# A causal mask by TensorE in the cross-attention stage, masked keys as one exponent per row, and no identity products between the transposes

## The chip, the cores and the metric

One core of a Trainium2 chip runs the whole program in one launch. The metric is the device time of the program in microseconds (us), the median of several runs. Engines: PE (TensorE), DVE (VectorE), ACT (ScalarE), POOL (GpSimd), and SP, which issues transfers.

## The reference, cut to what matters

Two layers, each an attention and a feed-forward part. The change is in the attention of the second layer: 8 batch rows, 256 queries and 256 keys, 512 features, 16 heads of 32. Queries are the normalised x; keys and values are the context itself, without projections.

```python
x = x + jnp.tanh(g_xattn[1]) * _L1_xattn_ref(_layernorm(x, axis=-1), ctx_2048, ctx_2048)
# in _L1_xattn_ref, with HEADS = 16, MASKED_BIAS = -10000.0:
scores = jnp.einsum('bhqd,bhkd->bhqk', qh, kh) / math.sqrt(hd)
causal = ki <= qi
scores = jnp.where(causal[None, None], scores, jnp.asarray(MASKED_BIAS, scores.dtype))
attn = jax.nn.softmax(scores, axis=-1)
out = jnp.einsum('bhqk,bhkd->bhqd', attn, vh)
```

The mask is -10000 and not minus infinity, so a masked key keeps a (tiny) share exp(-10000 - maximum), which the kernel computes too.

## The kernel before, in words

The program is seven stages, one after the other, with a barrier of all engines between them. The change is in stage 6, the function `cross`. It works on the eight batch rows in turns of two; in the code `b` is the row of a turn (a "batch" below, eight of them in all), `t` one of its two tiles of 128 queries, `h` a head, and `p` a pair of heads. A batch is eight steps `i`, one pair each. All engines run the same chain of steps (`chain` calls the `step(i, at, batch)` of each engine), in the order that their `step` functions write out; nothing but semaphores ties them together. Each engine executes its own instructions in order.

In a step with pair p:

- PE (`scores`, L1755 and L1758): four products with 32 rows, two heads by two query tiles, into the PSUM tensor `S[p % 2]` (two banks). The first query tile gets only its own 128 keys, the second all 256. It first waits until the exponentials of pair p-2 are done, since they read the same `S`. Then `turn_probs` for the second head of pair p-2, in even steps `values` (L1782, sixteen products for the four heads of two pairs), and `turn_probs` for the first head of pair p-1. `turn_probs` first multiplies the identity by itself into a part of the bank that nobody reads (L1764, two instructions in the trace), then waits for the head's exponentials, and turns three 128x128 blocks of probabilities (L1767).
- DVE (`maximum`): writes -10000 over the masked places of the two diagonal blocks of both heads with a predicated copy (L1915), then takes the negated maximum of each row (L1919).
- ACT: `exps` for the first head of pair p-1 (L1844, L1846, with the row sums), `keep_probs` (L1857, the copy of turned probabilities from PSUM) for the second head of pair p-2, `exps` for the second head of pair p-1, `keep_probs` for its first head.

Once a batch there is more. The first query tile's keys 128 to 255 are all masked and were never scored; their share is one exponent per row and head (`exps_apart`, L1851), times the sum of those keys' values, which PE makes with a product of ones by the second half of the context (`second_values`, L1743, step 1, into the PSUM bank `M`) and DVE copies out (L1910). DVE adds that share to the sums, inverts them (`over_sums`, L1926 to L1933, step 1); POOL makes `ev` from it (L1693) and adds it to x (`xe`, L1699, step 3), and adds the outputs (`y`, L1706, steps 4 and 5). DVE also takes the next batch's layer norm statistics (L192 to L197, step 2), normalises it (L204, step 4), scales the outputs (L1940, steps 3 and 4) and copies the second half of the next queries (L1905, step 6). PE turns the outputs (L1792, steps 3 and 4) and the next x (L1737, steps 5 and 6) through the same bank `M`. SP loads at step 1 and stores at step 6. Before the first steps PE runs 12 identity products at a time (L253).

## Time and profile before

| | |
|---|---|
| median of 3 runs | 2247.9 us (2247.34 to 2250.03) |
| the profiled execution: its own time, its span | 2249.69, 2247.9 us |
| mean granted clock of PE | 0.963 |
| busy over the span: PE, DVE, ACT, POOL | 89%, 61%, 48%, 19% |
| the cross stage, from 1828 to 2070.7 us: PE, DVE, ACT, POOL busy | 209.98, 182.65, 175.32, 51.68 us |

The profile is of one execution of the program. "Busy" is the time in which an engine has an instruction at work; PE's matmuls overlap and their ends are modelled, so a group of them can last longer in the trace than until the next group starts. Starts are therefore better to read than durations on PE. Behind a line of a timeline stands, in brackets, how long the engine idled before it and what released it. The granted clock (PEclk) is a share of 2.4 GHz, 0.50 is the lower level of 1.2 GHz.

### The profile page before, as it was taken

What the parts mean: (1) busy time and instruction counts of PE and PEld (TensorE: products, weight loads), DVE (VectorE), ACT (ScalarE), POOL (GpSimd) and SP (SyncE); (2) the same over time, 40 slices, a digit from 0 to 9 for tenths busy, and PEclk for the clock granted to TensorE, in tenths of its full rate; (3) what the DMA queues carried; (4) which work ended last, traced back from release to release, by engine and by line L of the source; (5) the groups of instructions that cost most, each with busy time, mean ns of one, the idle gap of its engine ahead of it and who ended that gap; (6) DMA issues with size and microseconds to landing.
All of it is one profiled execution on the core that took longest, in us unless ns stands there. A gap on an engine that the chain in (4) does not pass through costs nothing. (4 is left out here: it accounts for less than half of the span.)

```text
span 2247.9 us, 33557 instructions
## 1 busy us (share of the span) xinstructions
PE 1996.2 (89%) x10802; PEld 1531.6 (68%) x10818; DVE 1371.1 (61%) x2400; ACT 1073.3 (48%) x2593; POOL 425.4 (19%) x504
## 2 busy tenths in 40 slices
PE   6999479999989999987997999999689979997898
PEld 5888357776767677766886778778578866665454
DVE  6777266666666666663323764554544328885786
ACT  3333156666656666653113412121134318885898
POOL 1111034444444444430000000000000001222110
PEclk9999789999999999998998999999899989998999
DMA  5665662323232321006443221112295322321111
GB/s 213 243 243 231 244 178 76 98 64 103 60 101 76 85 76 48 22 27 239 145 136 137 83 75 38 56 37 57 62 339 198 118 81 68 113 94 48 48 56 43
DMA packets 192217, 250.42 MB, mean 111 GB/s; under 512 B 11574, under 2 KB 143814, under 8 KB 181836
## 3 DMA queue, kind: packets, MB, share of 16 engines
q1 hardware_dynamic: 192076, 248.67, 33.9%
q8 instruction: 72, 1.18, 0.2%
q14 instruction: 69, 0.57, 0.1%
HBM read 152.14 MB, written 96.48 MB: 111 GB/s over the span
## 5 line engine op out<-in xcount | busy, mean ns | idle before, releaser
L930 ACT ACTIVATE at_prob<-at_S,at_bias,at_rq 128x384 f32<-128x384 f32 (+1 forms) x256 | 184.2, 731 | 165.3 <-DVE at_bias L1016 159.1
L1027 DVE TENSOR_TENSOR at_pt_lo<-at_PT,at_pt_hi 128x512 fp32r<-128x512 f32 x224 | 148.8, 688 | 92.6 <-ACT at_pt_hi L937 92.6
L798 POOL TENSOR_SCALAR at_prob<-at_prob,at_rsum 128x384 f32<-128x384 f32 (+1 forms) x256 | 160.3, 639 | 174.7 <-DVE at_rsum L1022 174.7
L1444 ACT ACTIVATE gu_silu<-gu_G 128x512 f32<-128x512 f32 x64 | 38.3, 598 | 269.6 <-PE gu_G L103 260.1
L857 PE MATMUL at_PT<-c_ident,at_prob 128*128 128x128 f32 x896 | 127.8, 277 | 44.1 <-DVE at_pt_lo L1027 44.1
L937 ACT ACTIVATE at_pt_hi<-at_PT 128x512 fp32r<-128x512 f32 x224 | 127.9, 604 | 53.1 <-PE at_PT L857 53.1
L1007 DVE TENSOR_REDUCE at_nmax<-at_S 128x1 f32<-128x384 f32 (+1 forms) x256 | 147.7, 615 | 4.7 <-PE at_S L850 4.2
L857 PEld LDWEIGHTS at_PT<-c_ident,at_prob 128*128 128x128 f32 x896 | 97.7, 140 | 75.6 <-DVE at_pt_lo L1027 71.2
L1477 DVE TENSOR_TENSOR gu_h<-gu_silu,gu_U 128x512 f32<-128x512 f32 x64 | 43.9, 687 | 154.6 <-PE gu_U L103 109.7
L846 PE MATMUL at_S<-at_k_hi,at_q_hi 128*128 128x384 f32 (+1 forms) x256 | 112.7, 440 | 16.6 <-DVE at_q_lo L1032 13.4
L789 POOL TENSOR_TENSOR at_rq<-at_qv,c_minus_half 128x4 f32<-128x4 f32 x64 | 65.1, 1017 | 288.0 <-DVE at_qv L1002 288.0
L101 PE MATMUL gu_G<-gu_n_hi,gu_g_hi 128*128 128x512 f32 x256 | 103.0, 402 | 14.2 <-DVE gu_n_lo L1466 14.2
L101 PE MATMUL at_Q<-at_wq_hi,at_xt_hi 128*128 128x512 f32 x256 | 108.4, 423 | 7.1 <-issue 4.2
L213 POOL TENSOR_TENSOR x_rstd<-x_ve,c_minus_half 128x2 f32<-128x2 f32 x8 | 9.0, 1121 | 520.0 <-DVE x_ve L197 520.0
L101 PE MATMUL gu_U<-gu_n_hi,gu_u_hi 128*128 128x512 f32 x256 | 101.0, 395 | 5.9 <-DVE gu_h L1477 4.6
L103 PE MATMUL at_Q<-at_wq_lo,at_xt_hi 128*128 128x512 f32 x256 | 103.2, 403 | 0.0
L1172 PE MATMUL d_Y<-d_w_hi,d_a_hi 128*128 128x512 f32 x256 | 101.6, 397 | 1.7 <-DVE d_a_lo L1263 1.7
L102 PE MATMUL at_Q<-at_wq_hi,at_xt_lo 128*128 128x512 f32 x256 | 102.6, 401 | 0.0
L103 PE MATMUL gu_G<-gu_n_lo,gu_g_hi 128*128 128x512 f32 x256 | 102.6, 401 | 0.0
L102 PE MATMUL gu_G<-gu_n_hi,gu_g_lo 128*128 128x512 f32 x256 | 102.5, 401 | 0.0
L1172 PE MATMUL o_Y<-o_w_hi,o_a_hi 128*128 128x512 f32 x256 | 99.8, 390 | 1.7 <-DVE o_a_lo L1263 1.7
L102 PE MATMUL gu_U<-gu_n_hi,gu_u_lo 128*128 128x512 f32 x256 | 100.3, 392 | 0.0
(272 smaller groups left out, 5658.5 us busy)
## 6 DMA issues: line engine op xcount, KB each, us to landing
wide<-at_ot SPq DMA_DIRECT2D x64, 256.0 KB, 2.9
wide<-gu_h SPq DMA_DIRECT2D x64, 256.0 KB, 3.2
o_a<-wide SPq DMA_DIRECT2D x14, 1024.0 KB, 4.8
d_a<-wide SPq DMA_DIRECT2D x14, 1024.0 KB, 4.8
keys_hi<-kv_kt_hi SPq DMA_DIRECT2D x8, 1024.0 KB, 4.0
keys_lo<-kv_kt_lo SPq DMA_DIRECT2D x8, 1024.0 KB, 6.0
values_hi<-kv_v_hi SPq DMA_DIRECT2D x8, 1024.0 KB, 8.0
values_lo<-kv_v_lo SPq DMA_DIRECT2D x8, 1024.0 KB, 9.6
```

The costliest lines, as they stand in the source:

```text
L101: pe.matmul(out, wh, xh, start=(start and k == 0), stop=False)
L102: pe.matmul(out, wl, xh, start=False, stop=False)
L103: last = pe.matmul(out, wh, xl, start=False, stop=(stop and k == len(terms) - 1))
L789: pool.tensor_tensor(rq[u % 4][:], qv[u % 2][:], c.minus_half[:, 0:GROUP], ALU.pow).then_inc(rq_ready.sem, 1)
L798: pool.tensor_scalar(prob[u % 2][:, h, 0:n], prob[u % 2][:, h, 0:n], rsum[:, s:s + 1], 1.0, ALU.mult, ALU.mult).then_inc(normed.sem, 1)
L846: pe.matmul(S[h][:, 0:n], q_hi[u % 2][:, own], keys, start=True, stop=False)
L857: last = pe.transpose(bank_of("p", u, kb)[:, h * P:(h + 1) * P], prob[u % 2][:, h, kb * P:(kb + 1) * P], c.ident[:])
L930: act.activation(prob[u % 2][:, h, 0:n], S[h][:, 0:n], ACT.Exp, bias=bias[:, s:s + 1], scale=rq[u % 4][:, h:h + 1], accum_out=sums[:, s:s ...
L937: act.activation(pt_hi[f % 4][:], bank_of("p", u, kb)[:], ACT.Copy).then_inc(pt_hi_done.sem, 1)
L1007: dve.tensor_reduce(nmax[:, s:s + 1], S[h][:, 0:blocks[u] * P], AX_X, ALU.max, negate=True).then_inc(max_done.sem, 1)
L1027: dve.tensor_tensor(pt_lo[f % 4][:], bank_of("p", u, kb)[:], pt_hi[f % 4][:].bitcast(F32), ALU.subtract).then_inc(pt_done.sem, 1)
L1172: pe.matmul(Y[r][:], a_hi[r][:, k, :], w_hi[:, k, :], start=(k == 0), stop=False)
```

## The change: what it does

- The mask is added on PE: after the four score products of a pair, two bf16 products of the identity by a table of 0 and -1e30 (one per head, 256 columns, both diagonal blocks) accumulate onto `S`, and only the second signals DVE. The predicated copy goes.
- The maximum is followed by a small operation that bounds it (128x4, `tensor_scalar`), so that a row with masked keys has a maximum of at least -10000.
- All masked keys of both query tiles are now taken apart: the exponent per row and head has 32 columns in place of 16, times a count per row; their values are sums over the later keys (`masked_values`: a table `later` by the context, one product more for the first tile), so three fp32 products of 512 columns a batch on PE in place of one, in steps 1 and 2, two copies on DVE in place of one, and `ev` and `xe` on POOL for both tiles.
- The identity products in `turn_probs` go (128 in all). Those of L253 stay.
- Tables are made on DVE at the start of the stage, and one more is loaded.

```diff
-        apart = mem.sb("apart", [P, H1])
-        apart_gain = mem.sb("apart_gain", [P, H1])
-        v1 = [mem.sb(f"v1_{b}", [P, D]) for b in range(2)]
+        apart = mem.sb("apart", [P, QT, H1])
+        apart_gain = mem.sb("apart_gain", [P, QT, H1])
+        vm = [mem.sb(f"vm{b}", [P, QT, D]) for b in range(2)]
         ev = mem.sb("ev", [P, D])
-        xe = mem.sb("xe", [P, D])
+        xe = mem.sb("xe", [P, QT, D])
         ot = mem.sb("ot", [P, DC, L])
         o = [mem.sb(f"o{i}", [P, D]) for i in range(2)]
         y = mem.sb("y", [P, TT, D])
         after = mem.sb("after", [P, P], I32)
-        masked = mem.sb("masked", [P, 4 * P])
+        after_f = mem.sb("after_f", [P, P])
+        later = mem.sb("later", [P, P])
+        mask_f = mem.sb("mask_f", [P, P])
+        mask = mem.sb("mask", [P, P], BF16)
+        count = mem.sb("count", [P, QT])
+        bound = mem.sb("bound", [P, 1])
+        masked = mem.sb("masked", [P, 1])
...
+            sp.dma_start(mask_f[:], io["c_diag_mask"]).then_inc(setup, 16)
...
-            def add_apart(turn, b):
+            def add_apart(turn, b, t):
                 by_head = "p (h d) -> p h d"
+                n = QT * b + t
                 pool.wait_ge(*apart_gained.at(turn, b + 1))
-                pool.wait_ge(*v1_kept.at(turn, b + 1))
-                pool.wait_ge(*xe_done.at(turn, b))
-                pool.tensor_tensor(ev[:].rearrange(by_head, h=H1), v1[b][:].rearrange(by_head, h=H1),
-                                   apart_gain[:].rearrange("p (h a) -> p h a", a=1).to_broadcast([P, H1, HD1]),
+                pool.wait_ge(*vm_kept.at(turn, n + 1))
+                pool.wait_ge(*xe_done.at(turn, n))
+                pool.tensor_tensor(ev[:].rearrange(by_head, h=H1), vm[b][:, t, :].rearrange(by_head, h=H1),
+                                   apart_gain[:, t, :].rearrange("p (h a) -> p h a", a=1).to_broadcast([P, H1, HD1]),
                                    ALU.mult).then_inc(ev_done.sem, 1)
-                pool.wait_ge(*ev_done.at(turn, b + 1))
+                pool.wait_ge(*ev_done.at(turn, n + 1))
                 pool.wait_ge(*x_arrived[b].at(turn, 16))
-                pool.wait_ge(*y_done.at(turn, QT * (b - 1) + 1))
-                pool.tensor_tensor(xe[:], x[:, QT * b, :], ev[:], ALU.add).then_inc(xe_done.sem, 1)
+                pool.wait_ge(*y_done.at(turn, n + 1 - QT))
+                pool.tensor_tensor(xe[:, t, :], x[:, n, :], ev[:], ALU.add).then_inc(xe_done.sem, 1)
             def add(turn, b, t):
                 if t == 0:
-                    pool.wait_ge(*xe_done.at(turn, b + 1))
                     pool.wait_ge(*y_stored[b].at(turn, 0))
+                pool.wait_ge(*xe_done.at(turn, QT * b + t + 1))
                 pool.wait_ge(*o_done.at(turn, QT * b + t + 1))
-                pool.tensor_tensor(y[:, QT * b + t, :], o[t][:], xe[:] if t == 0 else x[:, QT * b + 1, :],
-                                   ALU.add).then_inc(y_done.sem, 1)
+                pool.tensor_tensor(y[:, QT * b + t, :], o[t][:], xe[:, t, :], ALU.add).then_inc(y_done.sem, 1)
             def step(i, at, batch):
                 if i == 2:
                     for turn, b in batch(1):
                         ln.gpsimd(pool, turn, c.minus_half, b)
-                if i == 3:
+                if i in (2, 3):
                     for a in batch(-1):
-                        add_apart(*a)
+                        add_apart(*a, i - 2)
                 if i in (4, 5):
...
-                    pe.wait_ge(*v1_kept.at(turn, b))
+                    pe.wait_ge(*vm_kept.at(turn, QT * b))
...
-            def second_values(turn, b):
-                pe.wait_ge(*cx_arrived[b].at(turn, 16))
-                pe.matmul(M[:], c.ones[:], cx[:, QT * b + 1, :], start=True, stop=True).then_inc(V1_full.sem, 1)
+            def masked_values(turn, b, t):
+                if t == 0:
+                    pe.wait_ge(*cx_arrived[b].at(turn, 16))
+                    pe.wait_ge(*x_kept[1].at(turn, b + 1))
+                else:
+                    pe.wait_ge(*vm_kept.at(turn, QT * b + 1))
+                last = pe.matmul(M[:], later[:], cx[:, QT * b + t, :], start=True, stop=(t == 1))
+                if t == 0:
+                    last = pe.matmul(M[:], c.ones[:], cx[:, QT * b + 1, :], start=False, stop=True)
+                last.then_inc(VM_full.sem, 1)
...
-                              start=True, stop=True)
+                              start=True, stop=False)
                 for a in range(2):
-                    last = pe.matmul(S[p % 2][:, 2 * L * a + L:2 * L * (a + 1)], qt[b][rows[a], k, P:L],
-                                     kt[b][rows[a], k, :], start=True, stop=True)
+                    pe.matmul(S[p % 2][:, 2 * L * a + L:2 * L * (a + 1)], qt[b][rows[a], k, P:L],
+                              kt[b][rows[a], k, :], start=False, stop=False)
+                for a in range(2):
+                    diagonals = S[p % 2][:, 2 * L * a:2 * L * (a + 1)].rearrange("p (t l) -> p t l", t=QT)[:, :, 0:P]
+                    last = pe.matmul(diagonals, c.ident_bf[:],
+                                     mask[:].rearrange("p (a l) -> p a l", a=1).to_broadcast([P, QT, P]),
+                                     start=False, stop=True)
                 last.then_inc(S_full.sem, 1)
             def turn_probs(turn, h):
                 pe.wait_ge(*pt_done.at(turn, h - 1))
-                pe.matmul(PT[h % 2][:, 3 * P:4 * P], c.ident[:], c.ident[:], start=True, stop=True)
                 pe.wait_ge(*exp_done.at(turn, h + 1))
                 for stands, block in ((0, 0), (2, 1), (1, 2)):
...
-                if i == 1:
-                    for turn, b in batch(0):
-                        pe.wait_ge(*x_kept[1].at(turn, b + 1))
-                        second_values(turn, b)
+                if i in (1, 2):
+                    for a in batch(0):
+                        masked_values(*a, i - 1)
                 if i == 3:
                     for a in batch(-1):
                         for turn, b in batch(0):
-                            pe.wait_ge(*v1_kept.at(turn, b + 1))
+                            pe.wait_ge(*vm_kept.at(turn, QT * (b + 1)))
...
+            pe.wait_ge(tables, 7)
             chain(pe, step)
...
-                act.activation(apart[:], nmax[:, HEADS * b:HEADS * (b + 1), 0], ACT.Exp,
+                act.activation(apart[:], nmax[:, HEADS * b:HEADS * (b + 1), :].rearrange("p h t -> p t h"), ACT.Exp,
...
-            dve.wait_ge(setup, 16)
+            def make_tables():
+                dve.wait_ge(setup, 2 * 16)
+                dve.tensor_copy(mask[:], mask_f[:]).then_inc(tables, 1)
+                dve.tensor_copy(after_f[:], after[:]).then_inc(tables, 1)
+                dve.wait_ge(tables, 2)
+                dve.tensor_tensor(later[:], after_f[:], c.ident[:], ALU.add).then_inc(tables, 1)
+                dve.tensor_reduce(count[:, 1:2], after_f[:], AX_X, ALU.add).then_inc(tables, 1)
+                dve.wait_ge(tables, 4)
+                dve.tensor_scalar(later[:], later[:], -1.0, 1.0, ALU.mult, ALU.add).then_inc(tables, 1)
+                dve.tensor_scalar(count[:, 0:1], count[:, 1:2], float(P), None, ALU.add).then_inc(tables, 1)
+                dve.tensor_scalar(bound[:], count[:, 1:2], 0.5, 3e38, ALU.is_lt, ALU.mult).then_inc(tables, 1)
+                dve.wait_ge(tables, 7)
+                dve.tensor_scalar(bound[:], bound[:], -MASKED_L1, None, ALU.max).then_inc(tables, 1)
+                dve.wait_ge(tables, 8)
...
-            def keep_second_values(turn, b):
-                dve.wait_ge(*V1_full.at(turn, b + 1))
-                dve.wait_ge(*ev_done.at(turn, b - 1))
-                dve.tensor_copy(v1[b][:], M[:]).then_inc(v1_kept.sem, 1)
+            def keep_masked_values(turn, b, t):
+                dve.wait_ge(*VM_full.at(turn, QT * b + t + 1))
+                dve.wait_ge(*ev_done.at(turn, QT * (b - 2) + t + 1))
+                dve.tensor_copy(vm[b][:, t, :], M[:]).then_inc(vm_kept.sem, 1)
             def maximum(turn, p):
                 bank = S[p % 2][:].rearrange("p (a l) -> p a l", a=2 * QT)
-                wait_apart(dve, S_full, turn, p + 1, passed)
-                dve.copy_predicated(bank[:, :, 0:P],
-                                    after[:].rearrange("p (a l) -> p a l", a=1).to_broadcast([P, 2 * QT, P]),
-                                    masked[:].rearrange("p (a l) -> p a l", a=2 * QT)).then_inc(masked_done.sem, 1)
-                dve.wait_ge(*masked_done.at(turn, p + 1))
-                dve.tensor_reduce(nmax[:, 2 * p:2 * p + 2, :], bank, AX_X, ALU.max, negate=True).then_inc(max_done.sem, 1)
+                own = nmax[:, 2 * p:2 * p + 2, :]
+                dve.wait_ge(*S_full.at(turn, p + 1))
+                dve.tensor_reduce(own, bank, AX_X, ALU.max, negate=True).then_inc(seen_done.sem, 1)
+                dve.wait_ge(*seen_done.at(turn, p + 1))
+                dve.tensor_scalar(own, own, bound[:, 0:1], None, ALU.min).then_inc(max_done.sem, 1)
...
-                dve.wait_ge(*ev_done.at(turn, b))
-                dve.scalar_tensor_tensor(out=sums[:, QT * b, :], in0=apart[:], scalar=float(P), in1=sums[:, QT * b, :],
-                                         op0=ALU.mult, op1=ALU.add).then_inc(sums_done.sem, 1)
+                dve.wait_ge(*ev_done.at(turn, QT * b))
+                for t in range(QT):
+                    last = dve.scalar_tensor_tensor(out=sums[:, QT * b + t, :], in0=apart[:, t, :], scalar=count[:, t:t + 1],
+                                                    in1=sums[:, QT * b + t, :], op0=ALU.mult, op1=ALU.add)
+                last.then_inc(sums_done.sem, 1)
...
-                dve.tensor_tensor(apart_gain[:], gain[:, QT * b, :], apart[:], ALU.mult).then_inc(apart_gained.sem, 1)
+                dve.tensor_tensor(apart_gain[:], gain[:, own, :], apart[:], ALU.mult).then_inc(apart_gained.sem, 1)
...
                         over_sums(*a)
+                if i in (1, 2):
                     for a in batch(0):
-                        keep_second_values(*a)
+                        keep_masked_values(*a, i - 1)
...
             ln.normalise(dve, 0, X_full.at(0, 0), 0)
+            make_tables()
             keep_x(0, 0)
```

(`V1_full` and `v1_kept` become `VM_full` and `vm_kept` with two counts a batch, `masked_done` becomes `seen_done`, and `ev_done` and `xe_done` count tiles.)

## Rows read from the trace of the kernel before

**Rows 1.** Windows: stage, its start, a batch, a thin stretch (busy us, PEclk, DMA, GB/s).

```profile
1828.00:2070.70 242.70, 209.98 (x1880) 149.50 (x1880) 182.65 (x251) 175.32 (x673) 51.68 (x40) 0.95 0.27 88
1838.00:1844.00 6.00, 4.77 (x24) 4.21 (x23) 1.36 (x3) 1.75 (x2) 0.60 (x1) 0.67 0.47 135
1929.92:1956.03 26.11, 24.43 (x229) 17.07 (x228) 22.23 (x31) 21.63 (x85) 6.69 (x5) 1.00 0.31 102
1856.00:1862.00 6.00, 4.33 (x37) 3.19 (x37) 5.49 (x9) 4.37 (x17) 1.12 (x1) 1.00 0.02 4
```

**Rows 2.** PE's timeline over two steps and a half (start, us, what, idle before).

```profile
1926.78 0.49 PE L1755 MATMUL x_S<-x_kt,x_qt 32*128 32x128 f32 x4 [0.83 <-ACT x_prob L1846]
...
1927.64 0.49 PE L1764 MATMUL x_PT<-c_ident 128*128 128x128 f32 x2
1927.96 0.49 PE L1767 MATMUL x_PT<-c_ident,x_prob 128*128 128x128 f32 x3
1928.38 0.86 PE L1782 MATMUL x_O<-x_pt,x_cx 128*32 128x256 f32 x16
...
1929.92 0.49 PE L1755 MATMUL x_S<-x_kt,x_qt 32*128 32x128 f32 x4
...
1931.65 0.49 PE L1767 MATMUL x_PT<-c_ident,x_prob 128*128 128x128 f32 x3
1931.97 1.02 PE L1743 MATMUL x_M<-x_cx,c_ones 128*128 128x512 f32 x2
```

**Rows 3.** ACT's timeline in the same batch.

```profile
1928.49 0.49 ACT L1857 ACTIVATE x_pt<-x_PT 128x384 f32<-128x384 f32 x1 [0.58 <-PE x_PT L1767]
1928.88 0.36 ACT L1844 ACTIVATE x_prob<-x_S,x_nmax 128x128 f32<-128x128 f32 x1
...
1929.67 0.31 ACT L1851 ACTIVATE x_apart<-x_nmax,x_masked 128x16 f32<-128x16 f32 x1
...
1940.28 0.37 ACT L1844 ACTIVATE x_prob<-x_S,x_nmax 128x128 f32<-128x128 f32 x1 [0.73 <-DVE x_nmax L1919]
```

**Rows 4.** DVE's timeline, at the stage's start and in the batch.

```profile
1843.64 0.69 DVE L1905 COPY x_qt<-x_M 128x512 f32<-128x512 f32 x1 [4.00 <-PE x_M L1737]
...
1931.00 0.70 DVE L1915 COPY_PREDICATED x_S<-x_after,x_masked 128x512 f32<-128x512 int32 x1 [1.18 <-PE x_S L1758]
1931.73 1.22 DVE L1919 TENSOR_REDUCE x_nmax<-x_S 128x4 f32<-128x1024 f32 x1
...
1938.29 0.70 DVE L1915 COPY_PREDICATED x_S<-x_after,x_masked 128x512 f32<-128x512 int32 x1
...
1943.60 2.18 DVE L204 TENSOR_SCALAR x_xn<-x_xl,x_mv,x_rstd 128x512 f32<-128x512 f32 x2
```

**Rows 5.** The chain that ended last: the bf16 products of the last stage.

```profile
2107.51 3.45 PE f_Y L2140 x16
```

**Rows 6.** POOL's timeline at the stage's end.

```profile
2060.82 1.05 POOL L1693 TENSOR_TENSOR x_ev<-x_v,x_apart_gain 128x512 f32<-128x512 f32 x1 [10.81 <-DVE x_apart_gain L1933]
2061.94 1.26 POOL L1699 TENSOR_TENSOR x_xe<-x_x,x_ev 128x512 f32<-128x512 f32 x1
2063.78 1.27 POOL L1706 TENSOR_TENSOR x_y<-x_o,x_xe 128x512 f32<-128x512 f32 x1 [0.57 <-DVE x_o L1940]
2065.60 1.26 POOL L1706 TENSOR_TENSOR x_y<-x_o,x_x 128x512 f32<-128x512 f32 x1 [0.55 <-DVE x_o L1940]
```

**Rows 7.** Lines 1915 and 1016 alone (duration ns min/median/max).

```profile
L1915 DVE COPY_PREDICATED x_S<-x_after,x_masked x64: 684/699/1710, 1845.5 to 2055.1; 128x512 f32<-128x512 int32 x64
...
L1016 DVE TENSOR_TENSOR at_bias<-at_nmax,at_rq x128: 160/162/1245, 298.5 to 1001.0; 128x2 f32<-128x2 f32 x128
```

**Rows 8.** SP's queue at the stage's start.

```profile
1830.65 0.34 SPq L1648 DMA_DIRECT2D x_after<-in_c_after_dram  x1
```

**Rows 9.** Four transposes on PE, at the start and in the batch.

```profile
1841.13 1.01 PE L1737 MATMUL x_M<-c_ident,x_xn 128*128 128x128 f32 x4
...
1942.27 0.60 PE L1792 MATMUL x_M<-c_ident,x_ot 128*128 128x128 f32 x4
```

More of the change, by code:

```diff
@@ L1588, in cross @@
         x_kept = [mem.counter(f"x_kept{t}", 2) for t in range(QT)]
-        V1_full = mem.counter("V1_full", 2)
-        v1_kept = mem.counter("v1_kept", 2)
+        VM_full = mem.counter("VM_full", TT)
+        vm_kept = mem.counter("vm_kept", TT)
         S_full = mem.counter("S_full", NP)
-        masked_done = mem.counter("masked_done", NP)
+        seen_done = mem.counter("seen_done", NP)
         max_done = mem.counter("max_done", NP)
@@ L1604, in cross @@
         apart_gained = mem.counter("apart_gained", 2)
-        ev_done = mem.counter("ev_done", 2)
-        xe_done = mem.counter("xe_done", 2)
+        ev_done = mem.counter("ev_done", TT)
+        xe_done = mem.counter("xe_done", TT)
         o_done = mem.counter("o_done", TT)
@@ L1611, in cross @@
         masks = mem.sem("masks")
+        tables = mem.sem("tables")
         passed = mem.sem("passed")
@@ L1724, in _ @@
         def _(pe):
-            for s in (X_full, V1_full, S_full, PT_full, PV_done, O_turned):
+            for s in (X_full, VM_full, S_full, PT_full, PV_done, O_turned):
                 s.start(pe)
@@ L1892, in _ @@
         def _(dve):
-            for s in (x_kept[1], v1_kept, masked_done, max_done, sums_done, rsum_done, gain_done, apart_gained, o_done,
+            for s in (x_kept[1], vm_kept, seen_done, max_done, sums_done, rsum_done, gain_done, apart_gained, o_done,
                       ln.stats, ln.xn_ready):
```

## The prediction, made before the changed kernel was run

> **What bounds the kernel now.** The change touches only the cross-attention stage, 243 of 2247.9 us (first line) [rows 1]. First the windows view: full granted clock in a typical batch of eight head pairs, 26.11 us long, with PE busy 24.43, DVE 22.23, ACT 21.63 (third line) [rows 1]. No engine is idle for long, so shares decide nothing, and I read one step (one pair) on each engine.
>
> PE's timeline [rows 2]: a step starts with the scores, which waited 0.83 us for the exponentials of two pairs back; 0.86 later come the identity products, 0.32 later the three transposes, 0.42 later the value products of two pairs (even steps only), then identity products and transposes of the second head; these three take 1.54 to the next scores, so the value products are 1.54 - 0.32 - 0.42 = 0.80. ACT [rows 3]: the copy of the turned probabilities starts 0.53 after the transposes began and had idled 0.58 for them; it takes 0.39 until the next exponentials, and these 0.79 per head. That is a closed loop: end of a head's exponentials, 0.17 to PE, scores 0.86, identity 0.32, transposes until ACT 0.53, copy 0.39, exponentials 0.79: 3.06 us. Even steps are also full on PE: 0.86 + 0.32 + 0.42 + 1.54 = 3.14, from the scores at 1926.78 to those at 1929.92. Eight loops would be 24.5 us. Counted out, a batch has four plain steps, the steps 1 and 2 (3.06 and 3.14), and two late ones, which get what is left: 26.11 - 3 x 3.06 - 3 x 3.14 = 7.5, or 1.4 over two loops. That is DVE [rows 4]: the maximum of pair 3 starts at 1938.29, behind the layer norm's statistics, and ACT idles 0.73 for it; that of pair 5 stands behind a normalisation of 2.18.
>
> DVE itself takes 0.73 for the predicated copy and 1.22 for the reduction, 1.95 a pair [rows 4]; in plain steps that is beside the loop, since DVE has idled 1.18 before. So **the 0.7 us that the change takes from DVE is mostly off the path**; only the two late steps see it.
>
> **Part by part.**
> *Identity products out.* 128 of them. The first of a step (0.32) is on the loop. The second is also on PE's path in even steps.
> *Mask products in.* Per pair two bf16 products of 256 columns with an identity as weights, ahead of the signal to DVE. No row has this shape. Lower end: 16 bf16 products of 512 columns took 3.45 us [rows 5], so 256 columns are 0.108, two are 0.22. Upper end: the fp32 identity product takes 0.32 in the same place, right behind the scores, while the second one of a step, behind other full-array work, takes 0.23 (1.73 from the scores at 1929.92 to the second transposes at 1931.65, less 0.86, 0.32 and 0.32) [rows 2]; so some 0.09 of it is the change-over, and a mask product has that to pay too, with smaller weights. I take 0.28. Then the loop goes from 3.06 to 3.02 (2.96 to 3.06): **one fill is replaced by another on the same spot.** Even steps need 1.14 + 0.42 + 0.80 + 0.42 = 2.78 on PE and fall back to the loop.
> *Masked values.* Before, one fp32 product of 512 columns a batch, in step 1: 1.02 us for its two instructions (the last row) [rows 2]; it just fitted. Now two such in step 1 and one in step 2. Step 1 on PE: scores 1.14, transposes 0.33 and 0.33 (the second took 0.32, from 1931.65 to 1931.97), products 2.0: 3.80, which is 0.78 over the loop. Step 2: 2.78 + 1.0 = 3.78, against 3.14. So +1.4 us a batch before anything is given back. DVE has a second copy of 0.69 (the queries' copy has its shape) (first line) [rows 4] and a second small sum.
> *What is queued behind the added wait.* In step 2 the second copy waits for its product, at the very end of PE's step, and behind it on DVE stand the statistics (some 2 us, which with the maximum before them make up the way to 1938.29) and the maximum of pair 3. By this schedule that maximum then ends 1.3 us later than before, counted from the scores of pair 1, though its own work is 0.5 shorter; PE is late by 1.1 too. So the saved DVE time shortens the two late steps only from 7.5 to about 7.1 together: nothing in the one behind the statistics but the loop's 0.04, 0.4 in the one behind the normalisation.
> *Batch:* four plain steps 12.08, then 3.80 + 3.78 + 7.1: 26.76 against 26.11, +0.64. Seven batches: +4.5. The first, without those extras, gets one product more in step 1 and loses little: +1.0.
> *The short DVE operation on the maxima.* 128x4, some 0.16 (as the 128x2 one of [rows 7]), plus 0.05 for its wait, between maximum and exponentials; in plain steps hidden by DVE's 1.1 idle. But POOL now works longer: a second pair of ev and xe, 1.05 and 1.26 [rows 6]. DVE operations do wait for POOL here: the predicated copy went from 0.70 to 1.71, and a 128x2 operation of the attention stage from 0.16 to 1.25 [rows 7]. Both have two SBUF inputs; the new one has a tensor and a scalar. Bounds: 0, or up to 1.1 on some three pairs a batch, of which the path sees 0 to 0.6. I take 0.1, inside the 7.1.
> The Trainium skill ("SBUF — State Buffer", Who interferes with whom) says that a scalar operation in a two-port mode is fully blocked until the GpSimd one ends. By that rule the batch would be 27.2 and the whole 2259; the normalisation at 2.18 for two agrees with it, but no small one of this form over a POOL operation stands in this trace. I give it a quarter of the forecast's chance.
> *Tail.* After the last pair POOL does ev, xe, y, y; xe started at 2061.94 and y at 2063.78 and 2065.60, waiting 0.57 and 0.55 for DVE [rows 6]. With ev and xe again (2.3) between, the last y moves by 2.3 less these waits, plus 0.2 for longer sums: +1.5. The store and the last stage stand behind it.
> *Start.* One more table is loaded on SP ahead of the first x: the one before it took 0.34 of issue [rows 8], I take +0.5. The eight small table operations (some 1.7 us) lie in DVE's wait of 4.00 us before the first queries' copy (first line) [rows 4]; without that cover they would cost 1.7.
>
> **Sum:** 4.5 + 1.0 + 1.5 + 0.5 = +7.5. The profiled execution took 2249.69 for a span of 2247.9, so 1.8 lie outside the span, and it stands 1.8 above the median of the three runs; the same +7.5 on the median 2247.9 gives **2255.4 us**. What a measurement can tell from no change is about 0.2%, or 4.5 us: below 2243.4 is faster, above 2252.4 slower.
>
> **Rivals.**
> *A, the loop does get shorter (faster).* Place: scores to transposes on PE. If the mask products cost 0.22, the transposes find their weights loaded under them (0.33 in place of 0.42, the two runs of rows 2), and DVE's saved half microsecond brings the maxima of pairs 3 and 5 in time, a batch is 26.76 - 0.5 - 0.7 - 1.1 = 24.5 (to 25.2 if only two of the three come true): with the 3.0 of the rest, 2240 (2239 to 2245). It decides where a plain step falls below 2.9. For: ACT idles at exactly that spot. Against: steps 1 and 2 are set by PE's sum, whatever the loop. 0.20.
> *B, a draw.* The mask products at 0.22 but the masked values at full price: 8 x 0.06 less a batch, so +0.1 to +0.2 a batch, +4 in all: 2251 (2246 to 2252.4). For: the 0.09 of change-over may be the fp32 weights' alone. Against: the weights of the mask products are as wide. 0.25.
> *C, the change doesn't do what it says to the clock.* With the fills gone PE is less busy; if the granted clock fell to its lower level, 1.2 GHz, all PE work would stretch: four transposes took 1.01 us in the start, in a stretch with a granted clock of 0.67 (part of it at 1.2 GHz) (second line) [rows 1], against 0.60 in the batch [rows 9]. By 1.7, 23.7 us of PE work a batch become 40: +14 a batch, over 100 us, 2360. The trace is against it: a stretch with PE busy 4.33 of 6 us still has a clock of 1.00 (last line) [rows 1], and a batch of the new kernel would hold 23.7 of PE work (8 x 1.14, 16 x 0.38, 4 x 0.80, 3.0 and four groups of four transposes, 0.53 to 0.60 each) in 26.8. 0.04.
> The Trainium skill ("TensorE: Matmul & The Clock Gate", Part 4, PE-mode transpose) speaks against the change: transposes, it says, don't count as busy for the clock, and without the identity products much of what is left are transposes. By that rule the time is C's. What the trace shows doesn't decide it, since here fills stand between all transposes.
> The forecast itself, 2249 to 2262 by its bounds: 0.51.
>
> **Chances.** Faster 0.19 (A without its slow end), same 0.27 (B, that end, and 0.01 of the forecast), slower 0.54 (the rest of the forecast and C). The range takes in the forecast, B and the slow part of A, up to one us beyond the highest bound, and leaves out C and the rest of A, together under 0.2: 2242 to 2263.
>
> **What would show it.** Right: in the batch's windows PE stays near 90% busy at clock 1.00; steps 1 and 2 last 3.7 to 3.9 from scores to scores, plain steps 3.0; the maximum of pair 3 still starts late, now behind the second copy of masked values; ACT still idles for transposes; POOL's tail is 1.5 longer. Wrong: plain steps below 2.9, which would mean masks much cheaper than 0.28; masked value products below 0.9 each; a clock under 1.00 in the middle of the stage; the short operation taking over 0.3 beside POOL's work (then the time is above 2258).

## The result, and the profile after

| | before | after |
|---|---|---|
| median, eight runs each, same chip | 2247.62 us (2245.22 to 2251.05) | 2257.97 us (2254.43 to 2264.59) |
| ratio to before | | 1.0045, interval 1.0029 to 1.0061 |
| profiled execution, its span | 2249.69, 2247.9 us | 2259.62, 2257.8 us |
| mean granted clock | 0.963 | 0.961 |
| first scores, last scores of the stage | 1844.43, 2054.03 us | 1845.03, 2063.07 us |
| a batch after the first, but the last (mean of six) | 26.32 us | 27.07 us |

The changed kernel is slower by 0.45%. Where the 9.9 us of span went is read from the starts of the scores on PE, 64 of them: the start +0.6; the first batch 29.5 to 33.3, +3.8; six batches 0.75 each, +4.5; the last seven steps +0.1; from the last scores to the end of the program 193.87 to 194.73, +0.9. So over a third of it is in the first batch. Steps of one batch, from scores to scores, in both kernels:

```
step          0     1     2     3     4     5     6     7    batch
before      3.14  3.05  3.13  3.13  3.57  3.05  3.98  3.06   26.11
after       2.96  3.59  3.63  2.96  3.74  2.96  4.15  2.96   26.95
```

The windows view of the changed kernel (columns as in [rows 1]): a batch's length from step 1 of that batch on, as in [rows 1], and two stretches of the first batch. Behind them the same two stretches of the kernel before, and the first of them in mask_alone, a kernel of the experiments below.

```profile
1935.59:1962.54 26.95, 23.90 (x214) 14.78 (x214) 20.89 (x33) 21.59 (x85) 8.13 (x7) 1.00 0.31 99
1860.00:1866.00 6.00, 4.95 (x37) 2.98 (x37) 4.45 (x10) 3.99 (x17) 0.70 (x1) 0.70 0.02 4
1866.00:1872.00 6.00, 6.00 (x39) 4.24 (x33) 2.29 (x4) 3.55 (x14) 0.00 (x0) 0.50 0.25 87
...
1860.00:1866.00 6.00, 5.17 (x52) 3.60 (x51) 5.26 (x8) 4.99 (x21) 1.03 (x1) 1.00 0.02 4
1866.00:1872.00 6.00, 5.60 (x57) 4.00 (x56) 3.95 (x5) 5.67 (x21) 0.00 (x0) 1.00 0.25 87
...
1860.00:1866.00 6.00, 4.82 (x52) 3.12 (x50) 3.46 (x5) 5.04 (x20) 0.70 (x1) 1.00 0.04 8
```

First line: PE at full clock, busy 23.90 of 26.95 (89%, before 94%); POOL 8.13 in place of 6.69. Second and third: in the first batch the granted clock fell to its lower level, for some 10 us (1863 to 1872 at 0.50), where the kernel before (fourth and fifth) and mask_alone (last) had 1.00. In the third line PE is busy throughout, and ACT, short of input, only 3.55.

PE's timeline (columns as in [rows 2]), from a plain step over step 1 to step 2:

```profile
1932.63 0.49 PE L1771 MATMUL x_S<-x_kt,x_qt 32*128 32x128 f32 x4 [0.74 <-ACT x_prob L1866]
...
1933.49 0.39 PE L1778 MATMUL x_S<-x_mask,c_ident_bf 128*128 128x256 bf16 x2
1933.72 0.49 PE L1787 MATMUL x_PT<-c_ident,x_prob 128*128 128x128 f32 x3
...
1935.59 0.49 PE L1771 MATMUL x_S<-x_kt,x_qt 32*128 32x128 f32 x4
...
1936.68 0.85 PE L1787 MATMUL x_PT<-c_ident,x_prob 128*128 128x128 f32 x6
1937.37 1.02 PE L1756 MATMUL x_M<-x_cx,x_later 128*128 128x512 f32 x2
1938.23 1.02 PE L1758 MATMUL x_M<-x_cx,c_ones 128*128 128x512 f32 x2
1939.18 0.49 PE L1771 MATMUL x_S<-x_kt,x_qt 32*128 32x128 f32 x4
```

The two mask products take 0.23, from 1933.49 to the transposes at 1933.72, where the identity took 0.32. Step 1 has no gap: scores and masks 1.09, six transposes 0.69, the two products of 512 columns 0.86 and 0.95, together 3.59. That is PE's sum, as predicted; scores with masks and the two products are smaller than forecast, the transposes 0.03 larger.

DVE's timeline in steps 2 to 4 of that batch (it answers to [rows 4]):

```profile
1942.92 0.69 DVE L1945 COPY x_vm<-x_M 128x512 f32<-128x512 f32 x1 [0.96 <-PE x_M L1756]
1943.53 1.27 DVE L192 BATCH_NORM_STATS2 x_bn<-x_xl 128x6 f32<-128x512 f32 x2
...
1945.42 1.23 DVE L1951 TENSOR_REDUCE x_nmax<-x_S 128x4 f32<-128x1024 f32 x1
1946.68 0.65 DVE L1953 TENSOR_SCALAR x_nmax<-x_nmax,x_bound 128x4 f32<-128x4 f32 x1
1947.24 0.68 DVE L1976 TENSOR_TENSOR x_o<-x_M,x_gain 128x512 f32<-128x512 f32 x1
1947.84 1.21 DVE L1951 TENSOR_REDUCE x_nmax<-x_S 128x4 f32<-128x1024 f32 x1
1949.09 0.94 DVE L1953 TENSOR_SCALAR x_nmax<-x_nmax,x_bound 128x4 f32<-128x4 f32 x1
1949.94 0.68 DVE L1976 TENSOR_TENSOR x_o<-x_M,x_gain 128x512 f32<-128x512 f32 x1
1950.54 2.50 DVE L204 TENSOR_SCALAR x_xn<-x_xl,x_mv,x_rstd 128x512 f32<-128x512 f32 x2
1952.96 1.21 DVE L1951 TENSOR_REDUCE x_nmax<-x_S 128x4 f32<-128x1024 f32 x1
```

And POOL's at the same time (it answers to [rows 6], there at the stage's end):

```profile
1946.25 1.05 POOL L1703 TENSOR_TENSOR x_ev<-x_vm,x_apart_gain 128x512 f32<-128x512 f32 x1
1947.54 1.27 POOL L1709 TENSOR_TENSOR x_xe<-x_x,x_ev 128x512 f32<-128x512 f32 x1 [0.24 <-POOL x_ev L1703]
1948.95 1.05 POOL L1703 TENSOR_TENSOR x_ev<-x_vm,x_apart_gain 128x512 f32<-128x512 f32 x1
1950.08 1.27 POOL L1709 TENSOR_TENSOR x_xe<-x_x,x_ev 128x512 f32<-128x512 f32 x1
```

The copy waits for its product (0.96) and statistics and maximum stand behind it, as predicted. Not predicted was that the short bound operation (L1953) takes 0.65 and 0.94. Put the two views side by side: the one of 1946.68 ends at 1947.33, when the `ev` that began at 1946.25 is over (1947.30); the one of 1949.09 ends at 1950.03, again just as the second `ev` is over (1950.00). It is so in every batch from the second to the seventh: twelve of 0.64 to 0.95, each ending 0.01 to 0.03 behind an `ev`. The line alone (duration ns min/median/max), all 64 of them, and ACT's wait behind it:

```profile
L1953 DVE TENSOR_SCALAR x_nmax<-x_nmax,x_bound x64: 229/229/946, 1848.2 to 2065.6; 128x4 f32<-128x4 f32 x64
...
  ACT x_prob L1864: 20.4, 18
```

A median of 229 ns says harmless; the maximum says where to look. ACT waited for it 18 times, 20.4 us in all; in the kernel before it waited for the maximum 17 times, 17.7 us in all.

### The profile page after: what moved, and what is told of

Same layout as the page of the kernel before. It is cut to its first block and busy times, and to the rows that moved or that the text cites. A ratio compares the mean times of both kernels' runs of the same rounds, so it can differ in the third digit from the quotient of the medians.

```text
span 2257.8 us, 33470 instructions
## 1 busy us (share of the span) xinstructions
PE 1993.9 (88%) x10706; PEld 1515.5 (67%) x10722; DVE 1354.9 (60%) x2424; ACT 1073.2 (48%) x2593; POOL 438.3 (19%) x520
## 5 line engine op out<-in xcount | busy, mean ns | idle before, releaser
L1951 DVE TENSOR_REDUCE x_nmax<-x_S 128x4 f32<-128x1024 f32 x64 | 78.1, 1221 | 44.6 <-PE x_S L1778 44.3
```

The source lines that it names most:

```text
L1951: dve.tensor_reduce(own, bank, AX_X, ALU.max, negate=True).then_inc(seen_done.sem, 1)
```

## The experiments

Each ratio is to the kernel before, run on the same chip with the experiment: 1.0045 [1.0029, 1.0061] is the changed kernel's. Batches are a typical one of the profiled execution.

| kernel | median us | ratio, interval | batch us |
|---|---|---|---|
| ident_back | 2267.16 | 1.0090 [1.0077, 1.0103] | 28.4 |
| ident_out | 2251.30 | 1.0027 [1.0015, 1.0039] | 25.7 to 26.0, some 30 |
| no_bound | 2249.14 | 1.0005 [0.9997, 1.0014] | 25.5 |
| mask_alone | 2235.34 | 0.9942 [0.9930, 0.9955] | 24.2 |
| bound_reduce | 2247.19 | 0.9999 [0.9988, 1.0009] | 25.65 |
| late_copy | 2256.02 | 1.0036 [1.0023, 1.0049] | 26.6, some 28 |
| mask_alone_ident | 2251.45 | 1.0020 [1.0009, 1.0031] | 26.7 |
| ident_first | 2263.0 (one run) | | 27, one 31.6 |
| mask_10000 | 2235.16 | 0.9930 [0.9917, 0.9944] | 24.2 |
| product_early | 2245.00 | 0.9982 [0.9972, 0.9991] | 25.0 |

**no_bound.** The changed kernel without the bound on the maxima (it leaves out the case of a row whose kept scores all lie below -10000):

```diff
-                dve.tensor_reduce(own, bank, AX_X, ALU.max, negate=True).then_inc(seen_done.sem, 1)
-                dve.wait_ge(*seen_done.at(turn, p + 1))
-                dve.tensor_scalar(own, own, bound[:, 0:1], None, ALU.min).then_inc(max_done.sem, 1)
+                dve.tensor_reduce(own, bank, AX_X, ALU.max, negate=True).then_inc(max_done.sem, 1)
```

> The changed kernel without the short operation that bounds the maxima (left out: the bound by which a row with masked keys has a maximum of at least -10000). Theory (it stands behind POOL's operations in the steps 3 and 4, up to 0.95 us, on the way from the maximum to the exponentials): the two late steps of a batch give back 0.6 to 0.9 us together, 5 to 7 us in all: 2251 to 2253. Rival (DVE is idle anyway, the copy and the statistics make the lateness): within 1.5 us of the changed kernel's 2258.

2258 falls to 2249.14, more than the 5 to 7 us expected: the small operation costs 9 us, 1.5 a batch. Steps 4 and 6 go from 3.74 and 4.15 to 3.21 each; steps 1 and 2 stay at 3.59 and 3.63. Step 4 is 3.21 although the second copy still stands ahead of statistics and maximum.

**ident_back.** The changed kernel with the identity products of the kernel before put back ahead of the transposes:

```diff
             def turn_probs(turn, h):
                 pe.wait_ge(*pt_done.at(turn, h - 1))
+                pe.matmul(PT[h % 2][:, 3 * P:4 * P], c.ident[:], c.ident[:], start=True, stop=True)
                 pe.wait_ge(*exp_done.at(turn, h + 1))
```

> The changed kernel with the 128 identity products put back ahead of the transposes, all else as changed. Theory (PE's sum and the loop scores, mask, transposes, copy, exponentials set the steps): each step gets 0.3 us longer, plain steps 3.2 to 3.3 in place of 2.96, some +15 to +19 us, less the 3 us that the clock dip in the first batch costs: 2270 to 2276, with a clock of 1.00 from 1856 us on. Rival (the missing fills are the loss, through the clock): the time falls back to 2250 or below.

Slower by 9 us, less than the 12 or more expected; plain steps 3.18 to 3.26 in place of 2.96, but the two late ones 3.70 and 3.76 in place of 3.74 and 4.15, though the bound operation lasts as long as before (0.64 to 0.96). The fills are 0.22 to 0.3 of the loop in every step. They do keep the clock: no stretch after 1850 us was below 1.00.

**ident_out.** The kernel before with only that line taken out.

> The kernel before with only the 128 identity products left out; mask by DVE and one masked value product as before. Theory: the loop falls from 3.06 to about 2.75 us a step, DVE becomes the bound in steps 1 to 5: batches of 24.5 to 25 us in place of 26.15, 2236 to 2242, with a clock dip somewhere in the first batches. Rival (clock): the clock falls again and again in the stage, and the time is at or above 2248.

Plain steps fell to 2.78, and batches without a dip of the clock to between 25.65 and 26.04, but the kernel was slower than before, 2251.30: the rival's time. The two late steps had grown to 3.88 and 4.60: with a shorter loop DVE, which still does 1.95 a pair, sets them (ACT idles 1.40 and 1.64 for its maxima there). Its windows:

```profile
1946.00:1952.00 6.00, 3.83 (x31) 2.37 (x23) 4.85 (x6) 5.18 (x21) 0.00 (x0) 0.76 0.47 142
1952.00:1958.00 6.00, 6.00 (x38) 3.40 (x38) 1.92 (x2) 3.83 (x16) 0.00 (x0) 0.50 0.23 70
1958.00:1964.00 6.00, 6.00 (x25) 3.31 (x27) 4.25 (x9) 2.60 (x12) 0.00 (x0) 0.50 0.00 0
```

For 12 us PE ran at 1.2 GHz, and that batch took 29.95; there was such a dip at 1872 to 1880 too (29.72), and a weaker one at 2030 to 2042. In the first line, in whose last 3 us the clock had already begun to fall, PE was busy 3.83, and its longest idle stretch was 1.23; a stretch of 1.24 idle from 2002.2 had no dip within 25 us behind it. So the fills were worth having in the kernel before, and they are not free where the clock holds.

**mask_alone.** The kernel before, without identity products, and with the mask by TensorE as in the change; masked values, maxima, `ev` and `xe` stay as before. It leaves out the masked keys of the diagonal blocks: they count nothing, where the reference gives them exp(-10000 - maximum).

```diff
+                for a in range(2):
+                    diagonals = S[p % 2][:, 2 * L * a:2 * L * (a + 1)].rearrange("p (t l) -> p t l", t=QT)[:, :, 0:P]
+                    last = pe.matmul(diagonals, c.ident_bf[:],
+                                     mask[:].rearrange("p (a l) -> p a l", a=1).to_broadcast([P, QT, P]),
+                                     start=False, stop=True)
...
-                dve.copy_predicated(bank[:, :, 0:P],
...
-                pe.matmul(PT[h % 2][:, 3 * P:4 * P], c.ident[:], c.ident[:], start=True, stop=True)
```

> The kernel before with the mask added by PE (the table of 0 and -1e30, so the masked keys of the diagonal blocks count nothing) and without the identity products; the masked keys' share is taken only for the first query tile's second half, with one product, one copy and one ev and xe a batch, as before, and no bound. Theory (the masked values' products and what waits behind them are the loss): all steps near 2.96, batches of 23.9 to 24.4, 2232 to 2237, the clock dip of some 3 us included. Rival (the mask products or the clock are the loss): 2246 or more.

The fastest by far, 0.6% below before: six steps of 2.96 and two of 3.21. A window over most of a batch:

```profile
1872.00:1896.00 24.00, 21.64 (x210) 13.93 (x208) 16.62 (x23) 21.31 (x84) 5.77 (x5) 1.00 0.32 111
```

Clock 1.00 with PE 90% busy, with no identity product; so it was from 1850 to 2040. The bf16 mask products stand in the same place of the loop and are 0.09 cheaper than the fp32 identity. By themselves the mask products don't keep the clock, since the changed kernel has them and its dip; what else does here was not told apart. The two late steps are 6.42 together, where ident_out had 8.48.

**bound_reduce.** The bound kept, but taken by a reduction over pairs (maximum, bound), which has no scalar operand; the second column is filled once:

```diff
+        seen = [mem.sb(f"seen{b}", [P, 2 * QT, 2]) for b in range(2)]
...
-                dve.tensor_reduce(own, bank, AX_X, ALU.max, negate=True).then_inc(seen_done.sem, 1)
+                dve.tensor_reduce(seen[p % 2][:, :, 0], bank, AX_X, ALU.max, negate=True).then_inc(seen_done.sem, 1)
...
-                dve.tensor_scalar(own, own, bound[:, 0:1], None, ALU.min).then_inc(max_done.sem, 1)
+                dve.tensor_reduce(own, seen[p % 2][:], AX_X, ALU.min).then_inc(max_done.sem, 1)
```

> The changed kernel with the bound taken by a second reduction (minimum over pairs of the negated maximum and the bound, 128x4 out of 128x4x2) in place of the scalar operation; the result is the same. Theory (the bound itself is cheap, its scalar form waits until POOL's operation ends): the reduction never lasts over 0.3 us, the two late steps fall from 3.75 and 4.15 to 3.3 to 3.5 each, 2250 to 2253. Rival (the loss is the longer chain of two dependent operations): it stays within 2 us of 2258.

2247.19, level with the kernel before and below the 2250 to 2253 expected: the change's whole loss goes, and nothing is left out. The line alone, then DVE's and POOL's timelines where those of the changed kernel are above:

```profile
L1957 DVE TENSOR_REDUCE x_nmax<-x_seen x64: 160/161/164, 1847.3 to 2055.3; 128x4 f32<-128x8 f32 x64
```

```profile
1940.66 1.23 DVE L1955 TENSOR_REDUCE x_seen<-x_S 128x4 f32<-128x1024 f32 x1
1941.92 0.16 DVE L1957 TENSOR_REDUCE x_nmax<-x_seen 128x4 f32<-128x8 f32 x1
1942.04 0.69 DVE L1980 TENSOR_TENSOR x_o<-x_M,x_gain 128x512 f32<-128x512 f32 x1
...
1943.90 0.16 DVE L1957 TENSOR_REDUCE x_nmax<-x_seen 128x4 f32<-128x8 f32 x1
1944.33 0.69 DVE L1980 TENSOR_TENSOR x_o<-x_M,x_gain 128x512 f32<-128x512 f32 x1 [0.27 <-PE x_M L1813]
1944.93 2.02 DVE L204 TENSOR_SCALAR x_xn<-x_xl,x_mv,x_rstd 128x512 f32<-128x512 f32 x2
1946.87 1.21 DVE L1955 TENSOR_REDUCE x_seen<-x_S 128x4 f32<-128x1024 f32 x1
```

```profile
1941.49 1.05 POOL L1704 TENSOR_TENSOR x_ev<-x_vm,x_apart_gain 128x512 f32<-128x512 f32 x1
...
1944.20 1.05 POOL L1704 TENSOR_TENSOR x_ev<-x_vm,x_apart_gain 128x512 f32<-128x512 f32 x1
```

Never over 164 ns. The first reduction begins 0.43 behind the start of `ev` (1941.92, 1941.49), just as the scalar operation did (1946.68, 1946.25), and lies wholly beside it: the same place, 0.16 in one form and 0.65 in the other. The second is over before its `ev` begins. From the maximum of pair 3 to that of pair 5 DVE needs 6.21 (1940.66 to 1946.87) in place of 7.54 (1945.42 to 1952.96). The 1.33 are 0.44 to the first `o`, 0.41 to the second (0.27 of its gain went into a wait for PE), and 0.48 in the normalisation, which met POOL less badly. With nothing on POOL beside it, it takes about half of that, as in the changed kernel's first batch:

```profile
1865.84 1.00 DVE L204 TENSOR_SCALAR x_xn<-x_xl,x_mv,x_rstd 128x512 f32<-128x512 f32 x2
```

**late_copy.** The changed kernel, the second copy of masked values moved behind the statistics:

```diff
-                if i in (1, 2):
+                if i == 1:
                     for a in batch(0):
-                        keep_masked_values(*a, i - 1)
+                        keep_masked_values(*a, 0)
                 if i == 2:
                     for turn, b in batch(1):
                         ln.statistics(dve, turn, b)
+                    for a in batch(0):
+                        keep_masked_values(*a, 1)
```

> The changed kernel with the second copy of masked values behind the layer norm's statistics on DVE in place of ahead of them. The prediction's theory (the copy's wait of about 1 us holds up statistics and the maximum of pair 3): the maximum of pair 3 starts 0.5 us earlier and step 4 falls from 3.75 to 3.3, some -3 to -4 us in all. Rival (POOL's operations beside the bound make the step late): POOL starts earlier too, the bound waits as before, and the time stays within 1.5 us of 2258.

Step 4 fell from 3.74 to 3.21, but step 6 stayed at 4.2 and the whole gained only 2, between what the two sides expected, and the two intervals overlap. DVE's and POOL's timelines there:

```profile
1915.06 0.23 DVE L1953 TENSOR_SCALAR x_nmax<-x_nmax,x_bound 128x4 f32<-128x4 f32 x1
...
1917.69 0.23 DVE L1953 TENSOR_SCALAR x_nmax<-x_nmax,x_bound 128x4 f32<-128x4 f32 x1
...
1919.07 2.90 DVE L204 TENSOR_SCALAR x_xn<-x_xl,x_mv,x_rstd 128x512 f32<-128x512 f32 x2
```

```profile
1917.77 1.28 POOL L1709 TENSOR_TENSOR x_xe<-x_x,x_ev 128x512 f32<-128x512 f32 x1
1919.01 2.68 POOL L1716 TENSOR_TENSOR x_y<-x_o,x_xe 128x512 f32<-128x512 f32 x2
```

The bound operation now falls between POOL's and takes 0.23 both times. But POOL started earlier too, so its two `y` lie wholly over the normalisation, 2.90 in place of 2.50 (2.02 in bound_reduce). **The same collision only moved to another scalar operation.** The small gain isn't the collision's alone, though. Batches without a dip of the clock are 26.6 (before the move 27.05), and four of the seven later ones begin with a step of 4.35 at a lowered clock (down to 0.53 over 3 us) in place of 2.96. With one of 1.4 in the first batch the dips cost this execution 7.0, and the changed kernel 3.8, so that some 3 us of gain are hidden. With step 4 at 3.21 in no_bound, copy in front, the queue behind the copy's wait is not the cause.

**mask_alone_ident.** mask_alone with the identity products kept.

> The kernel with the mask by PE, one masked value product a batch and no bound, and the 128 identity products put back. Theory (the mask products are fill enough for the clock, the identity products cost their 0.25 to 0.3 a step): plain steps 3.2, batches near 26, 2250 to 2254 against the 2235 without them. Rival (they earn something through the clock): under 2247.

2251.45 against 2235.34: the fills cost 16 us of the faster form. And against the kernel before, adding the masks to the loop while taking 0.7 a pair from DVE loses 0.2%: plain steps are 0.13 longer, and the two late ones 7.40 in place of 7.55 to 7.90. So neither edit pays alone: without the fills +0.27% (ident_out), with the mask on PE beside them +0.20%, both together -0.58% (mask_alone). The shorter loop needs DVE's saving in the late steps (8.48 without it, 6.42 with it).

**ident_first.** The changed kernel with the identity products in the first batch alone:

```diff
+                if isinstance(turn, int) and turn == 0 and h < HEADS:
+                    pe.matmul(PT[h % 2][:, 3 * P:4 * P], c.ident[:], c.ident[:], start=True, stop=True)
```

> The changed kernel with the identity products only in the transposes of the first batch of the first turn. Theory (the clock dip from 1862 to 1872 us comes from too thin work on PE in the first batch): clock 1.00 from 1856 us on, the first batch 31.3 to 31.6 us long in place of 33.3. Rival (the dip comes from elsewhere and falls where it likes): a dip of 6 us or more again in one of the first two batches.

The dip of the first batch went (31.37 in place of 33.3, as expected), and one came in the sixth, where neither side expected it: 0.76, 0.50 and 0.89 in the three windows from 1982 to 2000, that batch 31.6. Nothing gained. One run, so its time stands for little; its windows show that a dip isn't tied to the start.

**product_early.** bound_reduce with the first product of the masked values (the table `later` by the first tile) issued one batch ahead, in step 7, so that step 1 has one of its two.

> bound_reduce with the first of the three masked value products of a batch moved to step 7 of the batch ahead, where PE waits 1.2 us for the exponentials. Theory (steps 1 and 2 are set by the sum of PE's work): step 1 falls from 3.59 to 2.96, step 2 stays at 3.63, step 7 stays at 2.96; batches of 25.0 in place of 25.65, some 4.5 us less: 2242 to 2244. Rival (step 1 is late for another reason, or step 7 has no room): 2246 or more.

Step 1 fell from 3.59 to 2.96 and step 7 grew by 0.05 to 0.1; a batch 25.0. 2245.00, 0.2% below before, with all of the change's computation; it lies between what the two sides expected. In the profiled execution the clock stayed at 1.00 from 1853 us to the end of the batches, and 2.9 us of dips that bound_reduce had in its first two batches are gone too, against 1.3 us more in the very first step, whose clock was lower. So its 2 us against bound_reduce aren't the moved product's alone.

**mask_10000.** mask_alone with the table clipped to -10000, so that a masked key of a diagonal block keeps exp(score - 10000 - maximum):

```diff
-            dve.tensor_copy(mask[:], mask_f[:]).then_inc(tables, 1)
+            dve.tensor_scalar(mask[:], mask_f[:], MASKED_L1, None, ALU.max).then_inc(tables, 1)
```

> As mask_alone (mask by PE, no identity products, one masked value product a batch, no bound), with a mask table of -10000 (as bf16) in place of -1e30, so that a masked key of a diagonal block keeps a share of exp(score - 10000 - maximum). All theories: the same instructions but one small one at the start, so 2232 to 2238 again, and faster than the kernel before by 0.4 to 0.7%.

The time of mask_alone. It is nearer to the reference than -1e30, yet not it: the score stays in a masked key's exponent. It beats both kernels, by 0.7% the one before.

## Why the prediction was right, and where it was not

The time was forecast at 2255.4 and came at 2257.97: the side and the size are right, and not all reasons. In the span, +7.5 was forecast and +9.9 came. Nearly all that is missing is in the first batch, +3.8 for +1.0; that the others fit (+4.6 for +4.5) is errors that cancel, so that the closeness is in part luck.

- **The loop, 3.06 to 3.02.** It became 2.96, the lower end. *The mis-sized term* is the mask products: 0.28 taken, 0.23 measured. The change-over price that I gave them isn't there, and the transposes behind them take 0.33 to 0.42 as before. Four plain steps: 0.24 less than forecast.
- **Steps 1 and 2 at PE's sum, 3.80 and 3.78.** Right in mechanism: 3.59 and 3.63, below the 3.7 to 3.9 named as a sign but without a gap, and product_early takes 0.6 off step 1 by moving one product. A product of 512 columns costs 0.86 to 0.95 from start to start, not 1.0, and the mask's error is in here too. 0.36 less than forecast.
- **The short DVE operation, 0.1 inside the 7.1.** This is *the step that failed*: it was sized at 0.1 between bounds of 0 and 0.6, and costs 1.4 a batch (27.05 with it, 25.65 by a reduction). It took over 0.3 beside POOL's work, which the prediction itself had named as a sign of being wrong. The two late steps took 7.89, not 7.1; without the bound 6.42, where the forecast without it was 7.0. I had reasoned that three pairs a batch might meet POOL and the path see half of one delay. In fact two meet it, both are in DVE's one stretch without slack, and the delay pushes the normalisation onto POOL's next operations as well. Had it been 0 as its lower bound said, the change would have been level with before.
- **The rule I weighed against it.** The row shows 0.65 and 0.94 for 0.23, each ending with POOL's operation. The Trainium skill ("SBUF — State Buffer", Who interferes with whom) says that a scalar operation in a two-port mode is fully blocked while a GpSimd operation that was issued first holds the shared port pair. By that rule the 27.2 and 2259 worked out beside it were closer than my own (27.07 and 2257.97). The same section says that a reduction never contends on this chip, which is what bound_reduce shows (160 to 164 ns throughout). A quarter of the chance was too little.
- **What stands behind the second copy's wait.** Failed as a cause. The order is as I described it, 0.96 of waiting, but no_bound has it too and its step 4 is 3.21; late_copy removes it, and a batch gains only 0.4. The queue was also sized too long: from the scores of pair 1, the maximum of pair 3 was to end 1.3 later than before and ended 0.7 later (11.06 for 10.32, the bound not counted). That fits the 0.6 between 7.0 and 6.42.
- **The clock.** Rival C was wrong in size and not in kind: PE stayed at 1.00 in the batches, but in the first it was at the lower level for some 10 us. The sum gave this nothing. In product_early, at 1.00 there, steps 4 to 6 of the first batch take 9.13, in the changed kernel 12.97: the dip costs 3.8 us, over a third of the change's 9.9. (bound_reduce, whose dip there is shorter, 0.72 and 1.00 in the same two windows, has 30.85 in that batch in place of 33.3; no bound operation met POOL in it.) Every kernel here with identity products throughout kept 1.00 after 1850 us; of those without, mask_alone and mask_10000 had no dip in the batches and product_early none after 1853 us, bound_reduce and no_bound short ones up to 1880 us, late_copy and ident_out several. The Trainium skill ("TensorE: Matmul & The Clock Gate", Part 4, PE-mode transpose) speaks of transposes that don't hold the clock; the batches at 1.00 don't bear out a loss throughout, the dips in ident_out may be of that kind. PE had been less busy ahead of both dips at 0.50 (4.25 of the 6 us from 1943 to 1949 in ident_out, 1.95 of the 3 from 1860 to 1863 in the changed kernel). But mask_alone was as little busy in those 3 us (1.94) and kept 1.00, so what starts a dip stays open.
- **Start and tail.** +0.6 for +0.5; +0.9 for +1.5. POOL's last operations, `ev`, `xe`, `ev`, `xe`, `y`, `y`, ran almost back to back and ended 14.3 us after the last scores, before 12.8 (2065.60 + 1.26 from 2054.03 [rows 6]): the stage's tail is 1.4 longer, as forecast, and of it 0.6 was gained back behind the stage. The last batch grew by 0.1, not 0.64: it has no next batch's statistics and normalisation on DVE, and its step 4 fell from 3.57 to 3.21. (By their own terms the tail's sum is 1.4, not 1.5, and a batch's +0.65.)

The errors cancel: -0.24 and -0.36, then -0.6 for the queue and +1.4 for the bound, together +0.8 in the late steps, leave 26.95 for 26.76. Only the runs showed that one term was off by more than a factor of ten.

Rival A's mechanism, a shorter loop, is real: mask_alone has it, 24.2 a batch where A said 24.5. What kept it from the change is named by the runs: from mask_alone to no_bound the masked values and their tail cost 14 us (some 3 of them in two dips of the clock that mask_alone hasn't), and the bound another 9.

## What to carry to other kernels

Cost a new small operation by the form that it has and by what runs on POOL at that moment, not by its size, and read the maximum of its durations, not the median: here the same four numbers a row took 0.16 as a reduction and up to 0.95 as a scalar operation. Where a change bundles several edits, time its parts, singly and together: the mask by TensorE in place of the fills gained 0.6%, though each half of that swap alone lost 0.2 to 0.3%, and what was added beside it for masked keys lost 1%. In this kernel the fills were worth having only as long as no useful work stood in their place.

## What the runs showed of the hardware

- `tensor_scalar` of 128x4 beside POOL's `tensor_tensor`: 0.23 alone, 0.64 to 0.95 in the changed kernel when begun during an `ev`, and once 1.25 in late_copy, each time ending with POOL's operation; `tensor_reduce` to 128x4 from 128x8 0.160 to 0.164 always. The normalisation (two of 128x512) took 1.00 with nothing on POOL beside it and 1.95 to 2.93 otherwise, by where POOL was.
- Two bf16 products of 256 columns directly behind row-tiled fp32 ones: 0.23 together, and the fp32 identity in that place 0.32.
- The granted clock went to its lower level in the middle of the stage with no idle stretch of PE over 1.23 us ahead of it (ident_out), and stayed up in mask_alone. A batch with a long dip took 4 to 5 us more (29.95 for 26.04, 31.6 for 27), one with a short dip 1.4 more (28.0 for 26.6 in late_copy).
